# A graph network's convolution stage: node factors spread by DMA, layers written out, the last layer turned and stored group by group

## What is computed

```python
def _gcn_conv(x, src, dst, W, b, n_nodes):
    h = x @ W
    ...                                   # self loops are added to src, dst
    dis = where(deg > 0, rsqrt(deg), 0.0)
    msg = h[s] * (dis[s] * dis[d])[:, None]
    return segment_sum(msg, d) + b

h = max(layernorm(x), 0)
h = relu(batch_norm(gcn_conv(h, W1, b1), g1, be1))
h = relu(batch_norm(gcn_conv(h, W2, b2), g2, be2))
h = relu(gcn_conv(h, W3, b3))
h = gcn_conv(h, W3, b3)
return x + h
```

## Time and profile before

| | |
|---|---|
| median of 3 runs | 5498.39 us (5497.65 to 5499.48) |
| the profiled execution | 5488.85 us, span of its instructions 5487.0 us |
| PE busy | 4303.6 us, 78% |
| DVE busy | 2203.1 us, 40% |
| ACT busy | 1940.3 us, 35% |
| POOL busy | 1511.9 us, 28% |
| mean granted TensorE clock | 0.764 of full |
| node update | about 3530 to 3803 us |
| convolutions | about 3804 us to the end |

### The profile page before, as it was taken

The page is one execution under the profiler, slowest core; times in us unless marked ns, Lnnn a source line. Parts: engine busy times, 40 slices in busy tenths (PEclk is TensorE's granted clock), DMA queues, the critical chain, the costliest instruction groups (busy, mean ns, idle before and its releaser), DMA issues. The chain is left out here.

```text
span 5487.0 us, 70225 instructions
## 1 busy us (share of the span) xinstructions
PE 4303.6 (78%) x21902; PEld 2477.3 (45%) x21902; DVE 2203.1 (40%) x3441; ACT 1940.3 (35%) x5106; POOL 1511.9 (28%) x1604
## 2 busy tenths in 40 slices
PE   4477777777677777777777777577999999999998
PEld 3244444444444444444444444344444444444444
DVE  6455555555555555555555555554101101101101
ACT  2354555544455554445554445355001001001000
POOL 0344444444444444444444444100000000000000
PEclk7566666666766666666666676688999999999999
DMA  4222222222222222222222222201565565565564
GB/s 146 73 68 61 61 61 65 63 61 61 61 61 61 64 63 61 62 61 61 62 64 62 61 62 61 69 17 50 196 203 176 196 202 177 195 202 177 194 202 155
DMA packets 470358, 556.57 MB, mean 101 GB/s; under 512 B 38252, under 2 KB 417285, under 8 KB 470113
## 3 DMA queue, kind: packets, MB, share of 16 engines
q1 hardware_dynamic: 390880, 369.08, 20.8%
q0 software_dynamic: 51168, 107.68, 8.9%
q10 hardware_dynamic: 28224, 78.69, 3.8%
HBM read 453.73 MB, written 103.18 MB: 101 GB/s over the span
## 5 line engine op out<-in xcount | busy, mean ns | idle before, releaser
L788 POOL DMA_INDIRECT fts<-ft_tab,src_all x1568 | 1481.1, 945 | 1794.9 <-DVE terms L862 1373.4
L2035 PE MATMUL cv_acc<-cv_cnt,cv_parts 128*128 128x512 bf16 (+1 forms) x7056 | 1429.5, 366 | 0.0
L2035 PEld LDWEIGHTS cv_acc<-cv_cnt,cv_parts 128*128 128x128 bf16 x7056 | 666.0, 98 | 764.1
L825 DVE TENSOR_TENSOR ohk<-iota_ps,key_cols 128x784 bf16<-128x784 f32 x784 | 720.7, 955 | 0.0
L1069 PE MATMUL most_ps<-signs,most 1*128 1x2 f32 x392 | 107.0, 340 | 764.3 <-DVE most L834 713.9
L1088 PE MATMUL agg_ps<-terms,oh 128*64 128x141 f32 x2744 | 671.3, 434 | 2.5 <-DVE terms L862 2.5
L1088 PEld LDWEIGHTS agg_ps<-terms,oh 128*64 128x64 f32 x2744 | 584.0, 222 | 53.1 <-issue 37.7
L918 ACT ACTIVATE dist_l<-lo_iota,low 128x128 bf16<-128x128 f16 x1960 | 593.4, 387 | 7.0
L1026 PE MATMUL adj_ps<-ohk,ohl 128*128 128x196 bf16 x3136 | 593.5, 336 | 0.0
L1888 DVE TENSOR_TENSOR cv_y<-cv_acc,cv_dis_row 128x512 f32<-128x512 f32 (+1 forms) x52 | 34.4, 661 | 1353.8 <-PE cv_acc L2035 1325.2
L834 DVE TENSOR_REDUCE most<-most_ps 1x1 f32<-1x128 f32 x196 | 54.6, 279 | 1262.8 <-DMA key_rows<-edge_key,start_at 1255.2
(11 more groups left out here) (261 smaller groups left out, 3444.7 us busy)
## 6 DMA issues: line engine op xcount, KB each, us to landing
cv_cnt<-adj SPq DMA_DIRECT2D x96, 2048.0 KB, 8.0
cv_cnt<-adj SPq DMA_DIRECT2D x48, 2176.0 KB, 8.3
adj<-strip ACTq DMA_DIRECT2D x196, 392.0 KB
fts<-ft_tab,src_all POOLq DMA_INDIRECT x1568
win<-ft_tab SPq DMA_DIRECT2D x196, 65.0 KB
agg_tab<-res SPq DMA_DIRECT2D x196, 35.2 KB
cv_cnt<-adj SPq DMA_DIRECT2D x8, 512.0 KB, 3.7
agg_tab<-zero_f SPq DMA_DIRECT2D x5, 705.0 KB
```

Source lines behind the costliest of these rows:

```text
L788: nc.gpsimd.indirect_dma_start(fts[u][:, k, :], None, ft_tab[:, :], bass.IndirectOffsetOnAxis(src_all[:, n, k:k + 1], 0)).then_inc(gathere ...
L825: nc.vector.tensor_tensor(ohk[:, k.s, at, :], key_no.unsqueeze(1).to_broadcast([P, QC, KEYS]), columns(key_cols, k)[:, at].unsqueeze(2).to ...
L2035: last = nc.tensor.matmul(a[:, 0:width], parts[:, r, b, :], cnt[q][:, 0:width // SUB, (b - b0) * SUB:(b - b0 + 1) * SUB], start=(b == 0 an ...
```

## The change

Three edits.

1. `dis_row` now lives from the normalisation stage on. It is filled in the node update: SP stores `dis_col` to a small table in HBM, where the 49 values of a partition lie 512 bytes apart, waits for it, and loads the table back into all 128 partitions, ahead of the loads of `hn` for batches 2 to 6. The matmuls and copies that built it go.
2. The loop over layers is written out in Python on all engines; the loops over groups inside layers 0 to 2 stay. The masks go. Behind layers 0 and 1 the statistics chain is one link shorter, behind layers 2 and 3 it is gone, and `rectify` of layer 3 has no scale and shift.
3. In the last layer the groups are written out too. TensorE turns the tiles of group n-1 straight from `hT` behind the matmuls of group n, VectorE adds `x_sb` behind the next `finish_group`, and SP stores the rows of group i-3 behind the loads of the counts of group i. The stage copies of the end go. The general path keeps the old end.

```diff
 # node_update, SP
+                sp.dma_start(dis_tab.rearrange("(t p) -> p t", p=P), dis_col[:]).then_inc(dis_out, 16)
+            sp.wait_ge(dis_out, 16)
+            sp.dma_start(dis_row[:], row_bc(dis_tab)).then_inc(dis_in, 16)
             for i in range(2, NB):
                 sp.wait_ge(s["var1"], i - 1)
                 sp.dma_start(hn[i % 2][:], hn_dram[i * BW:(i + 1) * BW, :].rearrange("(b p) f -> p b f", p=P)
                              ).then_inc(hn_in[i % 2], 16)
+            sp.wait_ge(dis_in, 16)
 # convolutions, SP, last layer
+                        for i in range(NGR):
+                            counts_in(i, l * NGA + i, SPG, slice(i * SPG, (i + 1) * SPG))
+                            if i >= LATE:
+                                rows_out(i - LATE)
+                    counts_in(NGR, l * NGA + NGR, LW // SUB, slice(NGR * SPG, NS))
+                        for n in range(NGR - LATE, NGR + 1):
+                            rows_out(n)
 # VectorE
-            dve.wait_ge(s["row"], NB)
-            with dve.Fori(0, L) as l:
+            for l in range(L):
+                        for i in range(NGR):                   # last layer
+                            finish_group(...)
+                            if i:
+                                add_rows(i - 1)
+                        finish_group(...)                      # the group of 128
+                        add_rows(NGR - 1)
+                        add_rows(NGR)
+                if l < 2:
+                    ...
+                    ch(nc.vector.tensor_tensor(shift[:], tmp[:], bet[:, ds(l, 1)], ALU.add))
+                    settle(dve, s["y"])
+                    nc.vector.tensor_copy(scale[:], sd[:]).then_inc(s["ready"], 1)
+                elif l == 2:
+                    dve.wait_ge(s["y"], l * 7 + 1)
+                    settle(dve, s["ready"])
+                    def add_rows(n):
+                        dve.wait_ge(s["out_ps"], n + 1)
+                        if n >= 2:
+                            dve.wait_ge(out_done[n % 2], 16 * (n // 2))
+                        nc.vector.tensor_tensor(hs[n % 2][:, 0:w, :], x_sb[...], w_ps[n % 2][...], ALU.add
+                                                ).then_inc(s["sum"], 1)
 # ScalarE
-            for k in range(NB):
-                act.wait_ge(s["row_ps"], k + 1)
-                nc.scalar.copy(dis_row[:, k * BW:k * BW + 512], w_ps[k % 2][:, 0, :])
-                nc.scalar.copy(dis_row[:, k * BW + 512:(k + 1) * BW], w_ps[k % 2][:, 1, 0:384]).then_inc(s["row"], 1)
 # TensorE
-            for k in range(NB):
...
-                for b in range(BATCH):
-                    last = nc.tensor.matmul(w_ps[...], dis_col[...].to_broadcast([P, P]), ident[:], ...)
+                    def turn_rows(n):
+                        w = GRP // P if n < NGR else LW // P
+                        pe.wait_ge(s["dch"], l * NGA + n + 1)
+                        if n >= 2:
+                            pe.wait_ge(s["sum"], n - 1)
+                        for b in range(w):
+                            last = nc.tensor.transpose(w_ps[n % 2][:, 0, b * P:(b + 1) * P],
+                                                       hT[:, n * GRP + b * P:n * GRP + (b + 1) * P], ident[:])
+                        last.then_inc(s["out_ps"], 1)
+                        for n in range(1, NGA):                # last layer
+                            pe.wait_ge(acc_read[n % 2], l * uses[n % 2] + n // 2 + 1)
+                            group(l, l * NGA + n, acc[n % 2], n * (GRP // P), GRP if n < NGR else LW)
+                            turn_rows(n - 1)
+                        turn_rows(NGR)
```

More of the change, by code:

```diff
@@ L1453, in _ @@
                              ).then_inc(s["w_in"], 16)
+            with nc.allow_non_contiguous_dma(reason="one value per node, once"):
+                sp.dma_start(dis_tab.rearrange("(t p) -> p t", p=P), dis_col[:]).then_inc(dis_out, 16)
+            sp.wait_ge(dis_out, 16)
+            sp.dma_start(dis_row[:], row_bc(dis_tab)).then_inc(dis_in, 16)
             for i in range(2, NB):
@@ L1814, in _ @@
                                      ).then_inc(s["idx_in"], 16)
+                    if l == L - 1:
+                        with sp.Fori(0, NB // 2) as m:
+                            for u in range(2):
+                                sp.wait_ge(s["sum"], 2 * m + u + 3)
+                                sp.dma_start(out[ds((2 * m + u) * BW, BW), :].rearrange("(b p) d -> p b d", p=P), hs[u][:]
+                                             ).then_inc(out_done[u], 16)
+                        sp.wait_ge(s["sum"], NB + 2)
+                        sp.dma_start(out[(NB - 1) * BW:(NT - 1) * P, :].rearrange("(b p) d -> p b d", p=P),
+                                     hs[0][:, 0:BATCH - 1, :]).then_inc(out_done[0], 16)
+                        sp.dma_start(out[(NT - 1) * P:N, :], hs[0][0:N_LAST, BATCH - 1, :]).then_inc(out_done[0], 16)
+                        sp.wait_ge(out_done[0], 16 * (NB // 2 + 2))
+                        sp.wait_ge(out_done[1], 16 * (NB // 2))
@@ L1961, in _, with add @@
-            add(0, 0, 0, True)
-            add(1, 1, 0, True)
-            with dve.Fori(1, NB // 2) as j:
-                for u in range(2):
-                    add(2 * j + u, u, j, False)
-            add(NB - 1, 0, NB // 2, False)
+                    if l == L - 1:
+                        def add(k, u, j, first):
+                            dve.wait_ge(s["out_ps"], k + 3)
+                            if not first:
+                                dve.wait_ge(out_done[u], 16 * j)
+                            nc.vector.tensor_tensor(hs[u][:, 0:4, :], x_sb[:, ds(k * BATCH, 4), :],
+                                                    w_ps[u][:, 0, :].rearrange("p (b d) -> p b d", d=D), ALU.add)
+                            nc.vector.tensor_tensor(hs[u][:, 4:7, :], x_sb[:, ds(k * BATCH + 4, 3), :],
+                                                    w_ps[u][:, 1, 0:384].rearrange("p (b d) -> p b d", d=D), ALU.add
+                                                    ).then_inc(s["sum"], 1)
+                        add(0, 0, 0, True)
+                        add(1, 1, 0, True)
+                        with dve.Fori(1, NB // 2) as j:
+                            for u in range(2):
+                                add(2 * j + u, u, j, False)
+                        add(NB - 1, 0, NB // 2, False)
@@ L2055, in _ @@
             pe.sem_inc(s["hs"], 2)
-            with pe.Fori(0, L) as l:
+            for l in range(L):
                 def product(k, u):
@@ L2085, in _, with turn @@
                         last.then_inc(s["part_ps"], 1)
+                    if l == L - 1:
+                        pe.sem_inc(s["sum"], 2)
+                        def turn(k, u):
+                            pe.wait_ge(s["staged"], L * NB + k + 1)
+                            pe.wait_ge(s["sum"], k + 1)
+                            for b in range(BATCH):
+                                last = nc.tensor.transpose(w_ps[u][:, b // 4, (b % 4) * P:(b % 4 + 1) * P], stage[u][:, b, :],
+                                                           ident[:])
+                            last.then_inc(s["out_ps"], 1)
+                        with pe.Fori(0, NB // 2) as m:
+                            for u in range(2):
+                                turn(2 * m + u, u)
+                        turn(NB - 1, 0)
                 with pe.Else():
@@ L2099, in _ @@
-                    pe.wait_ge(acc_read[0], l * uses[0] + NGR // 2 + 1)
-                    group(l, l * NGA + NGR, acc[0], NGR * (GRP // P), LW)
-            pe.sem_inc(s["sum"], 2)
-            def turn(k, u):
-                pe.wait_ge(s["staged"], L * NB + k + 1)
-                pe.wait_ge(s["sum"], k + 1)
-                for b in range(BATCH):
-                    last = nc.tensor.transpose(w_ps[u][:, b // 4, (b % 4) * P:(b % 4 + 1) * P], stage[u][:, b, :],
-                                               ident[:])
-                last.then_inc(s["out_ps"], 1)
@@ L2111, in _ @@
-            with pe.Fori(0, NB // 2) as m:
-                for u in range(2):
-                    turn(2 * m + u, u)
-            turn(NB - 1, 0)
+                    def turn_rows(n):
+                        w = GRP // P if n < NGR else LW // P
+                        pe.wait_ge(s["dch"], l * NGA + n + 1)
[4 more added lines that the diff above has]
+                                                       hT[:, n * GRP + b * P:n * GRP + (b + 1) * P], ident[:])
+                        last.then_inc(s["out_ps"], 1)
```

181 lines of the change are left out of this document (87 added, 94 removed).

## The result

The changed kernel took **5468.5 us** (median of 5, 5466.25 to 5473.5) against 5499.48 us of the kernel before in the same session (5497.65 to 5503.61): a ratio of 0.9944, 95% interval 0.9929 to 0.9958. That is 31.0 us less, where 26.5 were forecast. The forecast of 5471.9 was 3.4 us too high.

What follows compares the result with a forecast made beforehand. TensorE's group matmuls were taken to bound the kernel, with gains only outside the groups. Terms -6.8 - 0.7 - 4.3 + 5.4 - 20.1 + 0 = -26.5 us took the median 5498.39 to 5471.9; range 5467 to 5477.

Steps and rivals of the forecast that it cites:

- Tail, E: Behind the last group matmul: most tiles are already out, so the end comes after 6.6 us, not 26.7; -20.1 us.
- The bound in which the 256 KB store holds the last one up: In the tail: the large store just ahead delays the last store by 2 us, leaving a gain of 18 us.
- Turns in the last layer, D: Eleven batches of four transposes on TensorE between the last layer's groups, 0.49 us each; +5.4 us, bounds 4.8 and 10.
- the 0.05 for waits: Last layer: three semaphore waits per batch of transposes, added to 0.44 us for the four transposes.
- Straight code at 0: Last layer's groups written out run without gaps on TensorE; cost 0, at most 1 us a group.
- Layers 0 and 1, B: Turns behind these layers: one chain link goes and the last becomes a copy, 2 x 0.37; -0.7 us.
- Layers 2 to 3, C: Turn behind layer 2: statistics chain goes, -2.8, and a higher clock gives 1.5 more; -4.3 us, bounds -2.6 and -4.8.
- 3 us is nearer to 2.2: Turn behind layer 2: TensorE idle 3 us returns at clock 1.00, as after 2.2 us, not 0.50; 1.5 us gained.
- Start, A: Start of the convolutions: spreading matmuls go, first product waits for parameters, at clock 0.50; -6.8 us, bounds -3 and -8.2.
- Factors in the node stage: Node stage: store of 21 us and spread under 25 fit a room of 66 us; cost 0, bounds 0 and +62.
- rival 1: Node stage: the store alone is slow, 55 us or more, 9 us beyond the room; 5481 us, chance 0.08.
- rival 2: Node stage: the spread crawls at single-row pace, 73 us, and VectorE stalls 28 us; 5500 us, chance 0.05.
- all three rivals: Node stage: slow store, slow spread, or both (5534 us, chance 0.04) make VectorE wait, one us per us beyond the room.

Runs made afterwards that it cites:

- e3: The changed kernel with the last layer's groups in their old loop and its rows turned, added and stored at the end; convolutions 1665.6 us against 1652.2.
- e5: The changed kernel with every transpose of the last layer issued twice; last layer 366.81 us against 362.01, convolutions 1657.4 us.
- e2: The kernel before with only the loop over layers written out, keeping masks, statistics chain and old end; 4150.1 us against 4153.1.
- e7: The changed kernel with unused matmuls keeping TensorE busy ahead of each layer's first products; convolutions 1648.6 us against 1652.2.
- e6: The changed kernel with the 12 parameter loads moved into the node stage behind the spread; convolutions 1647.0 us against 1652.2.
- e4: The changed kernel with store and spread of the factors made three times in a row; node stage 314.07 us, 41.1 more.
- e8: The changed kernel with early parameter loads, unused matmuls, split last store, no statistics in layers 2 and 3; 4115.85 us against 4156.6 for the kernel before.
- e10: The kernel of e8 without its unused matmuls; 5394.06 us against 5417.59 for the kernel before, convolutions 1645.5 us.
- e11: The kernel before, unaltered, run against itself; 5435.27 us against 5437.15, ratio 0.999.
- e12: The changed kernel, unaltered, in the session of e11; 5414.90 us against 5437.15 for the kernel before, ratio 0.9959.
- e9: The changed kernel, unaltered, in the session of e10; 5396.64 us against 5417.59 for the kernel before, ratio 0.9963.

## Why the prediction was right, and where it was not

**What bounds the kernel**: right. The groups run without a gap before and after, 31.73 us each, and everything that was gained lies outside them.

**Tail, E**: -20.9 for -20.1. The forecast put the last store's issue 2.35 us behind the last matmul and the end 4.2 behind that. They were 1.95 and 3.8: the two adds took 0.87 us together instead of 1.0, the statistics came 0.65 us behind the read instead of 0.76, and the last store ended 0.4 sooner. The bound in which the 256 KB store holds the last one up didn't occur. e3 adds a point on how a sum is read: 2.9 of these 20.9 us didn't need the turning, and the statistics chain in front and straight code gave them.

**Turns in the last layer, D**: +4.9 for +5.4. The transposes were priced rightly at 0.44 for four by the earlier trace rows; the 0.05 for waits was nothing. e5 shows the price to be that of the transposes alone. Straight code at 0: right. The first interval, written out but with no turn in it, is 31.73 us as in the loop; the next ten are 31.73 + 0.44 (32.16 or 32.17), and the last, with the narrow group, is 8.64 for 8.10.

**Layers 0 and 1, B**: the term that was mis-sized most, -2.65 for -0.7 and outside its bounds (0 to -1.5). The step that failed is "one link of the chain goes and the last becomes a copy, 2 x 0.37". The link did go, but the copy starts 0.15 us behind the one ahead of it (the scale of e2 0.04), and only 0.15 per turn remained (after against e2). What was missing is the loop itself: written out, with the same instructions, each turn is 1.1 to 1.25 us shorter (e2). I looked only for what leaving the loop could cost, a gap in straight code, and not for what the counter had cost. A hint was in the trace of before: of the small VectorE steps around, those with an operand that depends on the counter took 0.28 to 0.30 us from the one before, and the one without 0.19.

**Layers 2 to 3, C**: -5.2 for -4.3, beyond the bound of -4.8. The excess is straight code: against e2, which has it, the edit's own part is -4.15. To the first product it is -3.7, of which 1.05 is straight code (e2) and 2.66 the chain (forecast 2.8); TensorE stood idle for 2.05 us, not 3. Behind the first product it is -1.5, the size forecast for the clock, but not in the way forecast. Up to the first group matmul, where all 1.5 were to come, it is 1.0 (10.61 to 9.58). Another 0.3 is the second low stretch of before (3.10 us for 14 matmuls, 1.80 in after), which a reading of layer 0 doesn't have. And the clock was not 1.00: it was 0.74 and then 0.83, in part the lower level, with 5.02 us for the 28 product matmuls against 3.39 at 1.00. So a shorter low stretch gave the gain, not one that is gone. At 1.00, in e7, the way from the first product to the next read is 47.16 us in this turn, 47.76 in after and 49.25 in before. The cheaper `rectify` has hardly a share in it: e7's turn from 1 to 2, also at 1.00 but with scale and shift, has 47.26. The step that failed is "3 us is nearer to 2.2": the length of the idle time doesn't settle the clock. After 2.18 us it was 1.00, after 2.05 us it was in part at the lower level in after and, for the same 28 matmuls, at 1.00 in e6. That the size of this part came out all the same is luck.

**Start, A**: -7.2 for -6.8. The first product came 7.45 us behind the start ("near 8"), held by the parameters and at clock 0.50, 10.44 us from the first group. e6 shows by removal that it was the parameters.

**Factors in the node stage**: 0 for 0. The store took 22.9 us for 21 taken; the packet rate of the earlier trace rows was the right row, and the 55 us end (rival 1) was far off. The trace has 3.7 ns a piece, and three stores in e4 took 24.7, 24.0 and 27.5 us. The Trainium skill's DMA: Bandwidth & Descriptors, section on measured bandwidth, has about 10.5 ns a packet, for a 4 KB load issued from GpSimd; an estimate by that is 66 us for this store, which SP issues, and the measurement doesn't bear it out. The spread took 12.6 us, 255 GB/s on the mean, not the 44 GB/s of rival 2: that pace belongs to broadcasts of one 512-byte row. The load of hn, put at 3.6 us behind the spread, landed 1.1 us behind it. The mechanism of all three rivals is real (e4), it only starts 36 us further on.

**The whole**: the terms missed by -4.6 us in sum, B and C by -2.9 of it, where the one overlooked cause, straight code, is worth -3.4 in three turns. The profiled time of before lay 9.5 us below its median, and the difference was simply carried over; the convolutions' -31.1 matches the medians' -31.0 in the session of the result, and e8's -39.7 the -40.8 of its medians, but in the later sessions with the long attention stage the medians gave -21 and -22, and -23.5 for e10 with convolutions of -37.8.

## What to carry to other kernels

Work that stands in series behind a loop whose bounding engine never waits should be cut up and put between the loop's groups, even on that same engine: 0.44 us a group bought 18.0 us of tail (e3). At the turns between stages look at the gaps between small instructions, not only at their durations: the hardware loop over the layers, with the operands that depended on its counter, cost over 1 us per turn here. A slow strided store is free as long as what is queued behind its wait isn't needed yet, so work out that room before counting bytes. To it belongs the load itself: issued behind a large one it lands behind that (13.3 us here), and a median over several loads hides the one that counts.

## What was not expected of the hardware

**The same chip, 1280 us apart.** Chip 9 ran the kernel before in 4156.6 us in one session and in 5437.2 in a later one. Both windows are of the attention stage, from 1000 to 1080 us (busy PE, PEld, DVE, ACT, POOL, clock, DMA share, GB/s), first e8 in the early session, then e11 (the kernel before) in the late one:

```profile
1000.00:1080.00 80.00, 72.14 (x526) 47.77 (x527) 69.88 (x98) 65.41 (x187) 60.49 (x65) 0.90 0.40 104
```

```profile
1000.00:1080.00 80.00, 56.42 (x298) 35.88 (x299) 43.06 (x60) 40.86 (x111) 35.24 (x38) 0.67 0.23 62
```

In the late one every engine gets through 0.57 to 0.61 of the work, TensorE at a granted clock of 0.67 instead of 0.90 and with 0.189 us busy per matmul instead of 0.137. A gather on GpSimd takes the same 943 or 944 ns on the mean in both. The node stage starts at 2198 and at 3485. Clock alone would explain a ratio of 0.74; why it is less, and what sets the clock of a session, these runs don't show. It is no property of one chip, and the convolutions don't feel it (1652.3 us in e4, 1652.4 in e12).

**The clock between layers.** Filling TensorE's idle time kept the clock at 1.00 in one turn and only delayed the lower level in another of the same program (e7). The turn from 2 to 3 had products in part at the lower level in after, e9 and e12 (5.02 us for 28 each time), and at 1.00 in e6 and e10 (3.39), with 2.05, 2.05, 2.05, 2.05 and 1.86 us of idle time in front. So what follows can't be read from the idle time of one turn, and what else decides these runs don't show.

**Small things.** A DMA of 106 rows to HBM, split into 96 and 10, ended the span 2.6 us behind its first issue and 2.1 behind its second (e8), against 3.8 for the one of 106 rows. Of the tail's -1.3 us about 0.2 is the missing statistics: the first of these stores is issued 1.77 us behind the read, the whole one of after 1.95. A load of 448 KB issued just behind the 3.21 MB spread took 13.3 us to land instead of 3.6, and 12.1 in e4.
